# Attention in a fused kernel: order of the norm, of the first loads and of the weights' splitting

## The chip, the cores and the metric

One core of a Trainium2 chip runs the kernel. Its engines work side by side, each in the order of its own program, and wait for each other by semaphores: PE (TensorE, matmuls), DVE (VectorE), ACT (ScalarE), POOL (GpSimd), and SP, which here only starts DMAs. The metric is the device time of one execution in microseconds (us), the median of several.

## The reference, cut to what matters

Two layers of cross attention and feed-forward network run over 64 sequences of 128 tokens with 256 values each. The change is in the first one alone:

```
x = x + _L0_xattn_ref(ctx_1024, _layernorm(x), Wq, Wkv, Wo, ln1_w, ln1_b, ln2_w, ln2_b)

# _L0_xattn_ref(x, latents, ...): 16 heads of 64, INNER = 1024
xn = _layernorm(x, ln1_w, ln1_b)
ln = _layernorm(latents, ln2_w, ln2_b)
q = ln @ Wq
k, v = split(concat([xn, ln], tokens) @ Wkv)     # 256 keys a sequence
w = softmax(q k^T / 8)                           # per head
out = (w v) @ Wo
```

`ctx_1024` gives the tokens `x` of this function, and the normed `x` of the model the latents; so the latents are normed twice. The three stages behind (routed experts, an alignment, a quantized convolution network) are not touched.

## The kernel before

`attention` works on 32 pairs of sequences, p = 0 to 31, and cuts the 16 heads into four quads. A round u handles one quad of one pair (u = 4p + i), as two units n = 2u and 2u + 1, one a sequence; there are 128 rounds. The rounds are a software pipeline: in round u, PE makes the scores of round u, weighs the values of round u - 1 (`weigh_values`), projects k, q and v of round u + 1, and turns (transposes) the probabilities of round u. All matmuls with weights are made in three passes over a high and a low part of each operand, so every operand is split: ACT writes the high part, and a subtraction makes the low part, on DVE for q, k and the heads, on POOL for the inputs (`low_inputs`).

PE's results go to seven PSUM banks taken in turn. The order of the takes is written out by hand (`take`), and each take waits until the bank's user of seven takes before is done; for q that is `q_split`, raised by DVE's `low_q`. The second half of `turn_probs(2u + 1)` takes the bank that held q of round u + 1.

In the first round of a pair (i = 0) the norm of the next pair is made: `norm_a` (statistics of x and ctx on DVE, after which POOL's `inverse_std` makes the reciprocal deviations), `norm_b` (subtract and multiply, statistics of the latents), `norm_c` (second norm of the latents). In that round PE also makes the output of the pair before (`output`, 24 matmuls a sequence), and it ends with `turn_inputs`, which transposes the normed inputs of the next pair and waits for `normed`. ACT's `split_inputs` follows.

In the opening, SP loads 8 sequences of x, the norm columns, ctx of the first pair, and six pieces of 512 KB of weights (Wq, then Wkv's k and v halves) through four stages that lie in the yet empty end of `x_all`. DVE makes both parts of each piece (`split_weight`: a copy, L525, and a subtraction, L526). PE projects q, k, then v. Two pieces of Wo follow in the first round: DVE splits them between `row_max` and `invert`, and POOL's divide (L650) of the probabilities waits for `invert`.

Of the kernel before, what the change touches and what calls it, by code (L numbers as in the profile page):

```python
# [71 lines left out]
def attention(nc, dve_step, pool_step, x_all, ident, half, x, ctx, wq, wkv, wo, ln_cols):  # L72
# [10 lines left out]
    X_SETS = (range(0, 1), range(1, 2), range(2, 4), range(4, 8))  # L83
    STAGES, PER_STAGE = 4, INNER // DIM
    FREE_XC = (SEQS - STAGES * PER_STAGE) // XC
    MO = INNER // P
    with Stage(nc, "attention") as st:
# [28 lines left out]
        const_made, w_split = st.sems("const_made", "weights_split")  # L116
# [56 lines left out]
        for b in range(2):  # L173
            take("in", b, kv_scaled, 2 * b + 2)
        take("q", 0, q_split, 1)
        for c in range(2):
            take("k", c, k_split, c + 1)
        for c in range(2):
            take("v", c, v_copied, c + 1)
# [24 lines left out]
        def x_set(c):  # L204
            return next(i for i, chunks in enumerate(X_SETS) if c in chunks)

        def load_x(sp, c):
            sp.dma_start(x_all[:, XC * c:XC * c + XC, :], x[XC * c:XC * c + XC].rearrange("b t d -> t b d")
                         ).then_inc(x_loaded[x_set(c)], 16)

        def sp_program(sp):
            load_x(sp, 0)
            sp.dma_start(cols[:, :, :], ln_cols).then_inc(cols_loaded, 16)
# [21 lines left out]
            for c in range(FREE_XC, SEQS // XC):  # L235
                load_x(sp, c)
# [3 lines left out]
        def pe_program(pe):  # L240
# [58 lines left out]
            def project_v(c):  # L299
# [3 lines left out]
                pe.wait_ge(kv_split, 4 * p + 4)  # L303
# [66 lines left out]
            for c in range(2):  # L370
                project_v(c)
# [22 lines left out]
        def act_program(act):  # L394
# [61 lines left out]

            for b in range(2):
                split_inputs(b)
            high_q(0)
            for c in range(2):  # L460
                high_k(c)
            for c in range(2):
                copy_v(c)
            for u in range(ROUNDS + 1):
# [9 lines left out]
                if more:  # L474
# [3 lines left out]
                    copy_v(n + 3)  # L478
                if late_input(u) is not None:
                    split_inputs(late_input(u))  # L480

        def dve_program(dve):
# [18 lines left out]
            def norm_a(p):  # L501
                xs, cs, ls = pair(p)
                if 2 * p % XC == 0:
                    c = x_set(2 * p // XC)
                    dve.wait_ge(x_loaded[c], 16 * len(X_SETS[c]))
# [16 lines left out]
            def split_weight(n):  # L522
                src, hi, lo = staged[n]
                dve.wait_ge(stage_loaded[n % STAGES], 16 * (n // STAGES + 1))
                dve_step(dve, dve.tensor_copy(hi, stage_of(n)))  # L525
# [60 lines left out]
            for u in range(ROUNDS + 1):  # L586
# [18 lines left out]
                if norm_next:  # L605
                    norm_b(p + 1)
# [11 lines left out]
        def pool_program(pool):  # L618
# [23 lines left out]
            for b in range(2):  # L642
                low_inputs(b)
            for u in range(ROUNDS):
                p, i = divmod(u, QUADS)
                if p + 1 < PAIRS and not i:
                    inverse_std(p + 1, 0, 4)
                for n in (2 * u, 2 * u + 1):
# [3 lines left out]
                                       ).then_inc(divided, 1)  # L652
# [1525 lines left out]
```

## Time and profile before

| | |
|---|---|
| median of 3 runs | 3593.19 us (3592.61 to 3593.66) |
| the profiled execution | 3592.0 us, span 3590.3 us |
| PE busy | 3148.0 us, 88% of the span |
| DVE busy | 2499.0 us, 70% |
| ACT busy | 1830.2 us, 51% |
| POOL busy | 1352.1 us, 38% |

The span runs from the first to the last instruction of the profiled execution, and the rest of its time lies around it. Attention takes the time from 0 to about 1880 us. In the timelines the first number is the start in us from the span's start, the second how long the instruction or the merged run of them (xcount) took; square brackets tell how long the engine was idle before and who released it. PEld is PE's weight load.

### The profile page before, as it was taken

How to read it: one execution, taken by the hardware profiler on the slowest of the kernel's cores; microseconds unless marked ns; L12 is line 12 of the kernel's file. 1: busy time of each engine (PE TensorE's matmuls, PEld its weight loads, DVE VectorE, ACT ScalarE, POOL GpSimd, SP SyncE). 2: the span in 40 equal slices, each digit the busy share in tenths (PEclk: the TensorE clock that was granted, in tenths of full speed). 3: DMA queues.
4: the chain of work that ended last, by engine and by line, in shares of the span. 5: the costliest groups of instructions: out<-in, count | busy, mean ns of one | idle time of the engine just before them, and what ended most of it. 6: DMA issues, size and time to landing. Idle time of an engine off the chain costs nothing. (4 is left out here: it accounts for less than half of the span.)

```text
span 3590.3 us, 63845 instructions
## 1 busy us (share of the span) xinstructions
PE 3148.0 (88%) x23236; PEld 2704.7 (75%) x23236; DVE 2499.0 (70%) x5380; ACT 1830.2 (51%) x4693; POOL 1352.1 (38%) x1116
## 2 busy tenths in 40 slices
PE   6999999999999999999997999999999811177876
PEld 5888888888888888888886888888888710055655
DVE  6666666676666667676655665665664979789997
ACT  4555555556555555556553333333333612199996
POOL 2333333333333333333322333333333200068887
PEclk9999999999999999999998999999999955598888
DMA  4000000000000000000002101111101740001101
GB/s 150 4 7 5 7 7 4 7 4 7 4 7 4 7 7 4 7 4 7 4 1 78 48 32 41 49 30 43 48 25 48 215 103 0 12 30 36 38 29 35
DMA packets 104166, 107.96 MB, mean 30 GB/s; under 512 B 7857, under 2 KB 85169, under 8 KB 103857
## 3 DMA queue, kind: packets, MB, share of 16 engines
q1 hardware_dynamic: 103856, 103.88, 9.9%
q8 instruction: 189, 3.10, 0.4%
q14 instruction: 121, 0.98, 0.1%
HBM read 90.75 MB, written 13.11 MB: 29 GB/s over the span
## 5 line engine op out<-in xcount | busy, mean ns | idle before, releaser
L650 POOL TENSOR_TENSOR attention_prob<-attention_prob,attention_inv_sums 128x1024 f32<-128x1024 f32 x256 | 481.3, 1902 | 388.3 <-DVE attention_inv_sums L556 388.3
L442 ACT ACTIVATE attention_prob<-attention_turns,attention_neg_max 128x256 f32<-128x256 f32 x1024 | 468.5, 482 | 172.5 <-DVE attention_neg_max L547 172.5
L1097 POOL TENSOR_TENSOR experts_hidden_lo<-experts_weighed,experts_hidden_hi 128x512 fp32r<-128x512 f32 x192 | 252.0, 1313 | 551.9 <-ACT experts_hidden_hi L920 551.9
L563 DVE COPY attention_probT<-attention_turns 128x512 f32<-128x512 f32 x512 | 329.2, 684 | 151.5 <-PE attention_turns L329 151.5
L547 DVE TENSOR_REDUCE attention_neg_max<-attention_turns 128x2 f32<-128x512 f32 x512 | 317.8, 683 | 46.0 <-PE attention_turns L319 45.0
L920 ACT ACTIVATE experts_hidden_hi<-experts_weighed 128x512 fp32r<-128x512 f32 x192 | 121.4, 632 | 424.2 <-DVE experts_weighed L1049 424.2
L433 ACT COPY attention_v<-attention_turns 128x512 f32<-128x512 f32 x256 | 150.8, 589 | 330.0 <-PE attention_turns L263 330.0
L329 PE MATMUL attention_turns<-ident,attention_prob 128*128 128x128 f32 x2048 | 272.7, 274 | 42.2 <-DVE attention_q_lo L529 27.4
L329 PEld LDWEIGHTS attention_turns<-ident,attention_prob 128*128 128x128 f32 x2048 | 239.7, 141 | 85.8 <-DVE attention_q_lo L529 34.5
L1044 DVE TENSOR_TENSOR experts_silu<-experts_silu,experts_spread 128x512 f32<-128x512 f32 x128 | 89.3, 698 | 260.7 <-ACT experts_silu L914 259.6
L637 POOL TENSOR_TENSOR attention_kv_lo<-attention_kv_full,attention_kv_hi 128x256 fp32r<-128x256 f32 x128 | 96.2, 752 | 456.7 <-ACT attention_kv_hi L411 456.6
L345 PE MATMUL attention_heads_out<-attention_probT,attention_v 128*64 128x128 f32 x4096 | 251.8, 276 | 1.0 <-DVE attention_probT L563 1.0
L407 ACT ACTIVATE attention_kv_full<-attention_turns,attention_ln_cols 128x128 f32<-128x128 f32 x256 | 102.3, 449 | 270.2 <-PE attention_turns L256 269.4
L345 PEld LDWEIGHTS attention_heads_out<-attention_probT,attention_v 128*64 128x64 f32 x4096 | 220.9, 137 | 18.2 <-DVE attention_probT L563 1.2
L556 DVE RECIPROCAL attention_inv_sums<-attention_row_sums 128x4 f32<-128x4 f32 x256 | 44.5, 174 | 265.9 <-ACT attention_prob L442 265.9
L442 ACT ACTIVATION_READ_ACCUMULATOR attention_prob<-attention_turns,attention_neg_max 128x1 f32 x1024 | 219.5, 214 | 0.0
L853 PE MATMUL experts_out<-experts_down_hi,experts_hidden_hi 128*128 128x256 f32 x768 | 217.6, 283 | 0.6 <-POOL experts_hidden_lo L1097 0.6
L853 PE MATMUL experts_out<-experts_down_hi,experts_hidden_lo 128*128 128x256 f32 x768 | 217.3, 283 | 0.0
L853 PE MATMUL experts_out<-experts_down_lo,experts_hidden_hi 128*128 128x256 f32 x768 | 216.9, 282 | 0.0
L295 PE MATMUL attention_turns<-attention_kv_hi,attention_wkv_hi 128*128 128x512 f32 x512 | 215.1, 420 | 0.0
L263 PE MATMUL attention_turns<-attention_wkv_hi,attention_kv_hi 128*128 128x512 f32 x512 | 213.1, 416 | 0.0
L529 DVE SCALAR_TENSOR_TENSOR attention_k_lo<-attention_turns,attention_k_hi 128x512 fp32r<-128x512 f32 x256 | 176.6, 690 | 44.7 <-ACT attention_k_hi L425 40.3
(265 smaller groups left out, 9883.0 us busy)
## 6 DMA issues: line engine op xcount, KB each, us to landing
experts_spread<-shares SPq DMA_DIRECT2D x256, 128.0 KB, 3.0
x_all<-in_x SPq DMA_DIRECT2D x8, 1024.0 KB, 10.4
attention_ctx<-in_ctx SPq DMA_DIRECT2D x32, 256.0 KB, 2.8
distance_ctx<-in_ctx SPq DMA_DIRECT2D x16, 512.0 KB, 4.4
distance_ctxT<-in_ctxT SPq DMA_DIRECT2D x32, 256.0 KB, 4.8
weights_ctx<-in_ctx SPq DMA_DIRECT2D x16, 512.0 KB, 3.9
out<-conv_x_out SPq DMA_DIRECT2D x15, 512.0 KB, 3.0
dist<-distance_dist SPq DMA_DIRECT2D x16, 256.0 KB, 2.5
```

The source lines that it names most:

```text
L263: made = pe.matmul(out, left[l](k), right[r](k), start=n == 0, stop=n == 3 * KD - 1)
L295: made = pe.matmul(bank[:, :].rearrange("p (e c t) -> p c e t", e=2, c=2), wkv_p[l][:, k, w:w + P], (kv_hi, kv_lo)[r][p % 2][:, k, :, :, : ...
L329: made = pe.transpose(bank[:, (2 * h + t) * P:(2 * h + t + 1) * P], prob[n % 2][:, 2 * g + h, t * P:(t + 1) * P], ident[:, :])
L345: made = pe.matmul(heads_out[o * HEAD:(o + 1) * HEAD, (QT * e + m) * TOK:(QT * e + m + 1) * TOK], v[:, home, e, t, h, :], probT[e][:, h, t ...
L433: act.copy(v[:, 0:2 + pj % 2:1 + pj % 2, e, t, :, :].rearrange("p q h c -> p q (h c)"), bank_of("v", c)[:, :].rearrange("p (q c) -> p q c" ...
L442: made = act.activation(prob[n % 2][:, h, :], bank_of("s", 2 * n + e)[:, m * 256:(m + 1) * 256], ACT.Exp, bias=neg_max[:, n % 2, 2 * e + m ...
L529: return dve.scalar_tensor_tensor(lo, view, scale, hi.bitcast(F32), ALU.mult, ALU.subtract)
L547: made = dve.tensor_reduce(neg_max[:, n % 2, 2 * e:2 * e + 2], bank_of("s", 2 * n + e)[:, :].rearrange("p (h c) -> p h c", h=2), AX.X, ALU ...
L563: dve.tensor_copy(probT[n % 2][:, 2 * g:2 * g + 2].rearrange("p h t c -> p (h t c)"), bank_of("t", 2 * n + g)[:, :]).then_inc(p_copied, 1)
L650: pool.tensor_tensor(prob[n % 2][:, :, :], prob[n % 2][:, :, :], inv[:, n % 2, :].unsqueeze(2).broadcast_to([P, QH, 2 * TOK]), ALU.mult).t ...
L853: made = pe.matmul(out_ps[i // 2][:, (i % 2) * DIM:(i % 2 + 1) * DIM], l[n % 3][:, i * TOK:(i + 1) * TOK], down_w[r][:, m, :], start=t == ...
L1097: pool.tensor_tensor(hid_lo[n % 3][:, :], weighed[n % 2], hid_hi[n % 3][:, :].bitcast(F32), ALU.subtract).then_inc(hid_split, 1)
```

## The change

It is in `attention` alone and leaves every value computed as it is.

- The norm of the next pair: in rounds with i = 0, DVE now does `low_q`, `low_k` and the copy of the first unit's probabilities, then `norm_b`, the second copy, `norm_c`. In the first round `norm_a` comes behind the first copy too, and POOL makes the first reciprocal deviations behind the divides.
- Smaller first loads: x comes as sequences 0 and 1, later 2 to 7, then eights (`X_LOADS`); sequences 8 and up wait for somewhat other groups of loads (`X_SETS`).
- The weights come in another order, v, q, k, and ACT makes their high parts (`high_weight`), DVE their low parts (`low_weight`), laced into the first norm. PE projects v first and needs only one sequence's inputs for each of its first parts. DVE also makes the low parts of the first pair's inputs (`low_first_inputs`).
- The output weights are split when the first round ends.

```diff
-    X_SETS = (range(0, 1), range(1, 2), range(2, 4), range(4, 8))
+    X_LOADS = ((0, 2), (2, XC), *((c, c + XC) for c in range(XC, SEQS, XC)))
+    X_SETS = ((0,), (1,), (2, 3, 4), (5, 6, 7, 8))
+    X_FIRST = {X_LOADS[loads[0]][0]: i for i, loads in enumerate(X_SETS)}
...
-        for src, dst, c in ((wq, wq_p, 0), (wkv, wkv_p, 0), (wkv, wkv_p, INNER)):
+        for src, dst, c in ((wkv, wkv_p, INNER), (wq, wq_p, 0), (wkv, wkv_p, 0)):
...
-        WQ, WK, WV, WO = KD, 2 * KD, 3 * KD, 3 * KD + 2
+        WV, WQ, WK, WO = KD, 2 * KD, 3 * KD, 3 * KD + 2
...
         def sp_program(sp):
+            load_x(0)
             load_ctx(0)
-            for n in range(WV):
+            sp.dma_start(cols[:, :, :], ln_cols).then_inc(cols_loaded, 16)
+            for n in range(WK):
                 load_weight(n)
-            for c in range(1, FREE_XC):
-                load_x(sp, c)
+            load_x(1)
             load_ctx(1)
-            for n in range(WV, WO):
+            for n in range(WK, WO):
                 load_weight(n)
+            for n in range(2, FREE_LOADS):
+                load_x(n)
...
             def project_v(c):
-                pe.wait_ge(kv_split, 4 * p + 4)
+                pe.wait_ge(kv_split, 4 * p + 2 * e + 2)
...
+            for c in range(2):
+                project_v(c)
             project_q(0)
             for c in range(2):
                 project_k(c)
-            for c in range(2):
-                project_v(c)
...
+            def high_weight(n):
+                act.wait_ge(stage_loaded[n % STAGES], 16 * (n // STAGES + 1))
+                act.activation(staged[n][1], stage_of(n), ACT.Copy).then_inc(w_high, 1)
+
+            for n in range(STAGES):
+                high_weight(n)
             for b in range(2):
                 split_inputs(b)
+                high_weight(STAGES + b)
+            for c in range(2):
+                copy_v(c)
             high_q(0)
             for c in range(2):
                 high_k(c)
...
                     copy_v(n + 3)
+                if not u:
+                    for m in range(WK, WO):
+                        high_weight(m)
...
+            def low_weight(n):
                 src, hi, lo = staged[n]
+                dve.wait_ge(w_high, n + 1)
                 dve.tensor_tensor(lo, stage_of(n), hi.bitcast(F32), ALU.subtract).then_inc(w_split, 1)
...
+            def low_first_inputs(b):
+                for k in range(KD):
+                    dve.wait_ge(kv_high, 2 * b + k + 1)
+                    dve.tensor_tensor(kv_lo[0][:, k, :, b, :], kv_full[k][:, :, :],
+                                      kv_hi[0][:, k, :, b, :].bitcast(F32), ALU.subtract).then_inc(kv_split, 1)
+
             norm_a(0)
+            low_weight(0)
             norm_b(0)
+            low_weight(1)
             norm_c(0)
-            for n in range(WV):
-                split_weight(n)
+            low_weight(2)
+            low_first_inputs(0)
+            low_weight(3)
+            low_first_inputs(1)
+            low_weight(4)
+            low_weight(5)
             low_q(0)
...
                     row_max(n + 1)
-                    if not u:
-                        for m in range(WV, WO):
-                            split_weight(m)
-                    if norm_next:
+                    if norm_next and u:
                         norm_a(p + 1)
                     invert(n)
                     invert(n + 1)
...
                 if u:
                     low_heads(u - 1)
-                if norm_next:
-                    norm_b(p + 1)
                 if more:
                     low_q(u + 1)
                     low_k(n + 3)
                 if u < ROUNDS:
                     copy_probs(n)
+                    if not u:
+                        norm_a(1)
+                    if norm_next:
+                        norm_b(p + 1)
+                    copy_probs(n + 1)
                     if norm_next:
                         norm_c(p + 1)
-                    copy_probs(n + 1)
+                if not u:
+                    for m in range(WK, WO):
+                        low_weight(m)
...
             inverse_std(0, 1, 2)
-            for b in range(2):
-                low_inputs(b)
             for u in range(ROUNDS):
                 p, i = divmod(u, QUADS)
-                if p + 1 < PAIRS and not i:
+                if p + 1 < PAIRS and not i and u:
                     inverse_std(p + 1, 0, 4)
                 ...
+                if not u:
+                    inverse_std(1, 0, 4)
```

## Rows read from the trace of the kernel before

**Rows 1.** The page's busy time and share of each engine, whole span.

```profile
PE 3148.0 (88%) x23236; PEld 2704.7 (75%) x23236; DVE 2499.0 (70%) x5380; ACT 1830.2 (51%) x4693; POOL 1352.1 (38%) x1116
```

**Rows 2.** Waits on PE, 0 to 1900 us: total us, times, longest us.

```profile
PE attention_turns L329 <- DVE attention_q_lo L529: 27.4, 30, 0.9
```

**Rows 3.** Timeline of DVE, a round with norm: start, us, engine, line, operation.

```profile
1027.28 2.76 DVE L497 TENSOR_SCALAR attention_latents<-x_all,attention_mean_var,attention_rstd 128x256 f32<-128x256 f32 x2
...
1031.68 0.66 DVE L529 SCALAR_TENSOR_TENSOR attention_q_lo<-attention_turns,attention_q_hi 128x512 fp32r<-128x512 f32 x1
...
1032.85 1.28 DVE L563 COPY attention_probT<-attention_turns 128x512 f32<-128x512 f32 x2
```

**Rows 4.** Timeline of DVE, 0 to 62 us.

```profile
7.60 0.75 DVE L489 BATCH_NORM_STATS2 attention_raw_stats<-x_all 128x6 f32<-128x256 f32 x2 [7.60 <-DMA attention_ctx<-in_ctx]
...
11.01 0.73 DVE L497 TENSOR_SCALAR attention_latents<-x_all,attention_mean_var,attention_rstd 128x256 f32<-128x256 f32 x2 [1.58 <-POOL attention_rstd L628]
...
14.62 0.74 DVE L497 TENSOR_SCALAR attention_latents<-attention_latents,attention_mean_var,attention_rstd 128x256 f32<-128x256 f32 x2 [1.16 <-POOL attention_rstd L628]
...
15.99 1.23 DVE L526 TENSOR_TENSOR attention_wq_lo<-x_all,attention_wq_hi 128x1024 fp32r<-128x1024 f32 x1
...
42.76 0.69 DVE L525 CAST attention_wo_hi<-x_all 128x1024 fp32r<-128x1024 f32 x1 [6.14 <-DMA x_all<-in_wo]
```

**Rows 5.** Timeline of POOL, the same round as rows 3.

```profile
1026.10 3.79 POOL L650 TENSOR_TENSOR attention_prob<-attention_prob,attention_inv_sums 128x1024 f32<-128x1024 f32 x2
```

**Rows 6.** Timeline of PE, the same round as rows 3.

```profile
1030.88 0.60 PE L329 MATMUL attention_turns<-ident,attention_prob 128*128 128x128 f32 x4
1032.39 0.66 PE L329 MATMUL attention_turns<-ident,attention_prob 128*128 128x128 f32 x4 [0.91 <-DVE attention_q_lo L529]
1033.08 0.36 PE L360 MATMUL attention_turns<-attention_wo_hi,attention_attT_hi 128*128 128x256 f32 x1
...
1038.90 0.27 PE L256 MATMUL attention_turns<-ident,attention_ctx 128*128 128x128 f32 x1
```

**Rows 7.** Timeline of PE, the round that starts at 59.11 us.

```profile
59.11 0.39 PE L319 MATMUL attention_turns<-attention_k_hi,attention_q_hi 64*128 64x256 f32 x2
...
70.55 1.03 PE L329 MATMUL attention_turns<-ident,attention_prob 128*128 128x128 f32 x8
71.42 0.27 PE L256 MATMUL attention_turns<-ident,attention_ctx 128*128 128x128 f32 x1
```

**Rows 8.** GB/s of the DMAs, 0 to 16 us, in 40 slices of 0.4 us.

```profile
GB/s 0 0 0 0 36 108 69 148 338 317 381 387 389 364 357 386 358 376 430 379 451 389 420 379 451 358 430 420 318 92 0 0 0 0 0 0 0 0 0 0
```

**Rows 9.** Timeline of ACT, 0 to 62 us.

```profile
7.00 1.28 ACT L407 ACT_TABLE_LOAD   x1 [7.00 <-DMA attention_ln_cols<-in_ln_cols]
```

**Rows 10.** ACT's groups by form: busy us, mean ns, idle us before.

```profile
L407 ACT ACTIVATE attention_kv_full<-attention_turns,attention_ln_cols 128x128 f32<-128x128 f32 x256 | 102.3, 449 | 270.2 <-PE attention_turns L256 269.4 <-POOL attention_kv_lo L637 0.8
...
L894 ACT ACTIVATE experts_xT_hi<-experts_xT 128x1024 fp32r<-128x1024 f32 x16 | 16.7, 1041 | 0.0
```

**Rows 11.** Timeline of PE, 0 to 62 us.

```profile
15.41 0.48 PE L256 MATMUL attention_turns<-ident,attention_ctx 128*128 128x128 f32 x1 [15.41 <-DVE attention_latents L497]
...
23.65 0.58 PE L263 MATMUL attention_turns<-attention_kv_hi,attention_wq_hi 128*128 128x256 f32 x1 [6.27 <-POOL attention_kv_lo L637]
...
26.38 0.63 PE L295 MATMUL attention_turns<-attention_kv_hi,attention_wkv_hi 128*128 128x512 f32 x1
...
28.82 0.40 PE L295 MATMUL attention_turns<-attention_kv_hi,attention_wkv_hi 128*128 128x512 f32 x1
...
33.10 0.39 PE L319 MATMUL attention_turns<-attention_k_hi,attention_q_hi 64*128 64x256 f32 x2
...
51.68 1.97 PE L329 MATMUL attention_turns<-ident,attention_prob 128*128 128x128 f32 x8 [11.16 <-POOL attention_prob L650]
```

**Rows 12.** Windows of 1 us: each engine's busy us (x), then PEclk, DMA, GB/s.

```profile
45.00:46.00 1.00, 0.00 (x0) 0.00 (x0) 0.97 (x2) 0.00 (x0) 0.00 (x0) 0.88 0.00 0
...
56.00:57.00 1.00, 1.00 (x9) 0.80 (x7) 1.00 (x2) 0.59 (x1) 0.52 (x1) 1.00 0.00 0
```

More of the change, by code:

```diff
@@ L81, in attention @@
     XC = 8
-    X_SETS = (range(0, 1), range(1, 2), range(2, 4), range(4, 8))
+    X_LOADS = ((0, 2), (2, XC), *((c, c + XC) for c in range(XC, SEQS, XC)))
+    X_SETS = ((0,), (1,), (2, 3, 4), (5, 6, 7, 8))
+    X_FIRST = {X_LOADS[loads[0]][0]: i for i, loads in enumerate(X_SETS)}
     STAGES, PER_STAGE = 4, INNER // DIM
-    FREE_XC = (SEQS - STAGES * PER_STAGE) // XC
+    FREE_LOADS = 1 + (SEQS - STAGES * PER_STAGE) // XC
     MO = INNER // P
@@ L115, in attention @@
         ctx_loaded, cols_loaded = st.sems("ctx_loaded", "cols_loaded")
-        const_made, w_split = st.sems("const_made", "weights_split")
+        const_made, w_high, w_split = st.sems("const_made", "weights_high", "weights_split")
         stats_made, rstd_made, normed = st.sems("stats_made", "rstd_made", "normed")
@@ L174, in attention @@
             take("in", b, kv_scaled, 2 * b + 2)
+        for c in range(2):
+            take("v", c, v_copied, c + 1)
         take("q", 0, q_split, 1)
@@ L177, in attention @@
             take("k", c, k_split, c + 1)
-        for c in range(2):
-            take("v", c, v_copied, c + 1)
         for u in range(ROUNDS + 1):
@@ L202, in bank_of, with load_x @@
             return turns[take_at[kind, n] % len(turns)]
[L204 to L209, printed above, removed]
         def sp_program(sp):
-            load_x(sp, 0)
-            sp.dma_start(cols[:, :, :], ln_cols).then_inc(cols_loaded, 16)
+            def load_x(n):
+                lo, hi = X_LOADS[n]
+                sp.dma_start(x_all[:, lo:hi, :], x[lo:hi].rearrange("b t d -> t b d")).then_inc(
+                    x_loaded[next(i for i, loads in enumerate(X_SETS) if n in loads)], 16)
             def load_ctx(p):
@@ L224, in load_weight @@
                 sp.dma_start(stage_of(n), staged[n][0]).then_inc(stage_loaded[n % STAGES], 16)
+            load_x(0)
             load_ctx(0)
-            for n in range(WV):
+            sp.dma_start(cols[:, :, :], ln_cols).then_inc(cols_loaded, 16)
+            for n in range(WK):
                 load_weight(n)
-            for c in range(1, FREE_XC):
-                load_x(sp, c)
+            load_x(1)
             load_ctx(1)
-            for n in range(WV, WO):
+            for n in range(WK, WO):
                 load_weight(n)
+            for n in range(2, FREE_LOADS):
+                load_x(n)
             sp.wait_ge(w_split, WO)
-            for c in range(FREE_XC, SEQS // XC):
-                load_x(sp, c)
+            for n in range(FREE_LOADS, len(X_LOADS)):
+                load_x(n)
             for p in range(2, PAIRS):
@@ L369, in pe_program @@
                 project_k(c)
-            for c in range(2):
-                project_v(c)
             for u in range(ROUNDS + 1):
@@ L455, in high_heads @@
                                ).then_inc(att_high, 1)
+            def high_weight(n):
[3 more added lines that the diff above has]
+                high_weight(n)
             for b in range(2):
                 split_inputs(b)
+                high_weight(STAGES + b)
+            for c in range(2):
+                copy_v(c)
             high_q(0)
@@ L461, in act_program @@
                 high_k(c)
-            for c in range(2):
-                copy_v(c)
             for u in range(ROUNDS + 1):
@@ L502, in norm_a @@
                 xs, cs, ls = pair(p)
-                if 2 * p % XC == 0:
-                    c = x_set(2 * p // XC)
-                    dve.wait_ge(x_loaded[c], 16 * len(X_SETS[c]))
+                if 2 * p in X_FIRST:
+                    i = X_FIRST[2 * p]
+                    dve.wait_ge(x_loaded[i], 16 * len(X_SETS[i]))
                 dve.wait_ge(ctx_loaded, 16 * (p + 1))
@@ L520, in norm_c @@
                 normalise(ls, ls, mv[1], rstd[1]).then_inc(normed, 1)
-            def split_weight(n):
+            def low_weight(n):
                 src, hi, lo = staged[n]
-                dve.wait_ge(stage_loaded[n % STAGES], 16 * (n // STAGES + 1))
-                dve_step(dve, dve.tensor_copy(hi, stage_of(n)))
+                dve.wait_ge(w_high, n + 1)
                 dve.tensor_tensor(lo, stage_of(n), hi.bitcast(F32), ALU.subtract).then_inc(w_split, 1)
```

## The prediction, made before the change was built or timed

> **What bounds the kernel now.** I read the engines' busy time first: PE (TensorE) is busy for 88% of the span, far above DVE (VectorE) and POOL (GpSimd) [rows 1]. So I looked at PE's idle time in attention with the view of waits, restricted to PE and to the first 1900 us. It has one line that repeats: 30 times, `turn_probs` (L329) waits for DVE's `low_q` (L529), 27.4 us in all, 0.9 us at most [rows 2]. Thirty is the number of rounds with u >= 1 in which the next pair's norm is made. The rest of PE's idle time in attention lies before the second round. Nothing else in attention repeats.
>
> The timeline of PE and DVE shows how the repeated wait arises. The last four transposes of `turn_probs(n+1)` need the PSUM bank that held q; it is free when `low_q` is done. DVE runs its program in order and has `norm_b` ahead of `low_q`. The first two subtractions of `norm_b` take 2.76 us there instead of 0.73 [rows 3, 4], while POOL runs its divides from 1026.10 to 1029.89 [rows 5]. `low_q` starts at 1031.68 and ends at 1032.34; PE resumes at 1032.39 [rows 3, 6].
>
> **The size of the wait.** From the first of these transposes to the first matmul behind them it is 1033.08 - 1030.88 = 2.20 us [rows 6]; in a round without the wait, 71.42 - 70.55 = 0.87 us [rows 7]. The difference is 1.33 us, more than the 0.91 shown as idle, because the view starts counting only when the modelled (pipelined) ends are past. I take 1.33, and keep 0.91 as the lower bound.
>
> **Part 1: the norm behind the queries.** Nothing is added or removed, DVE's order changes. `low_q` and `low_k` follow `low_heads` at 1027.3 and end about 1028.7 (two of 0.7). The bank is then free some 2.8 us before PE asks for it at 1031.3. Behind them comes `copy_probs(n)`: its transposes start about 2.3 before 1030.88, so the copy runs 1029.3 to 1030.6. `norm_b` starts at 1030.6, behind the divides. From `norm_b`'s start to `norm_c`'s start takes 3.61 us where nothing disturbs it, 1.16 of it waiting for POOL [rows 4]; `copy_probs(n+1)`, 1.28 us [rows 3], now lies in that wait, so `norm_c` starts near 1034.3 and ends near 1035.0. PE needs it for `turn_inputs`, at 1038.90 before [rows 6] and 1037.6 with the wait gone: 2.6 us in hand. The banks that `copy_probs(n+1)` frees near 1034.3 are wanted by the next scores at 1038.1. I find no new wait. Gain: 30 x 1.33 = 39.9 us; bounds 30 x 0.91 = 27.4 and 39.9.
>
> The Trainium skill (SBUF — State Buffer, "Who interferes with whom") says that a tensor_scalar in a 2-port mode and a GpSimd instruction shut each other out for a whole instruction, whoever is first. By that rule the 2.76 us are a block and go away when `norm_b` moves behind the divides; without the rule (2.76 kept) `norm_c` would end near 1037.1, still ahead of 1037.6, and the sum would be the same.
>
> **Part 2: the opening, up to the first score.** DVE starts at 7.60, when 1.31 MB (x, 8 sequences, and ctx) are in [rows 4]. By the row of GB/s [rows 8] 1.31 MB have moved by 6.4, so landing lags by about 1.1 us. Now only 0.52 MB are ahead: moved by 4.3, so DVE starts near 5.4 (5.0 to 5.6). But `low_weight(0)` stands before `norm_b` and waits for ACT, which waits for the first weight: 1.05 MB, moved by 5.7, landed near 6.8. The one table load takes 1.28 us and began at 7.00, at a DMA's landing [rows 9]; I place it behind the weight's wait (lower bound: before it, 1.28 less). Then 1.04 for ACT's copy [rows 10] and 1.23 for DVE's subtraction [rows 4]: `norm_b` starts near 10.4 instead of 11.01. `low_weight(1)` (1.23) fills the 1.16 wait for POOL. So `norm_c` starts near 14.1 and the transposes, 0.79 behind it as before (14.62 to 15.41 [rows 4, 11]), near 14.9. In `low_weight(1)`, DVE reads two SBUF tensors while POOL computes the rstd that is waited for; if POOL had to wait out the subtraction, 1.1 us more. Bounds 13.6 and 16.0; I take T = 15.2.
>
> Before, POOL made the low inputs, and the queries began 8.24 us after the transposes (15.41 to 23.65 [rows 11]). Now `project_v` needs only the first sequence: four transposes (1.1), two ACT scalings of two and two copies, six of about 0.45 [rows 10], and a short DVE subtraction: T + 4.1. From the first projection to the first score PE works 33.0 - 23.65 = 9.35 us, with matmuls of 512 columns at 0.63 us each at first and 0.40 from 28.8 on [rows 11]; this start comes after idle time too, so I keep 9.35. V first takes the first 5 us, in which the second sequence's input parts (about T + 7.5) and the K weights (about T + 9.9) are ready before Q and K want them. K is now last, so its high part (0.6) and low part (0.66 [rows 3]) and the hand-overs are exposed: 1.4 us that V covered before. First score: T + 4.1 + 9.35 + 1.4 = T + 14.9 = 30.1, against 33.10 [rows 11]. Gain 3.0 (bounds 2.2 and 4.6).
>
> **Part 3: the first round.** Before, `invert` stood behind the output weights, whose DMA landed at 42.76 [rows 4]; the round from score to score took 59.11 - 33.10 = 26.0 us [rows 7, 11]. Now with S the first score: PE is ready for the first transposes at S + 7.4 (before, it stopped 11.16 us ahead of 51.68 [rows 11], and 33.10 was S), the divide is done by then (no DMA ahead of it), and DVE copies the first probabilities from about S + 8.3 to S + 9.6. Then `norm_a(1)` to `norm_b` 3.41 us (7.60 to 11.01 [rows 4]), `norm_b` to `norm_c` 3.7 (with the copy in it), `norm_c` 0.74, transposes about 0.5: next score at S + 18.1. Gain 7.9, give or take 1. PE stands idle from S + 10.5 to S + 17.6, 7.1 us. Before, PE stopped near 40.5 and the granted clock fell to 0.50 (the 1.2 GHz level) at about 45.9, and rose to 1.00 about 4.3 us after PE resumed at 51.68 [rows 11, 12]. The same should happen here, with 4.3 us at half rate inside the second round: -2.1 us (bounds 0 and -2.2). The output weights' two low parts (1.23 each) make the second round's maxima about 1 us late; the divide there has more than 2 us before its transposes, so nothing. ACT's two high parts (1.04 each) lie in its idle time before `split_inputs`. The smaller x loads add one DMA issue, behind the weights. What is moved behind them, x 2 to 7 and ctx 1, is wanted near 40, and all has moved by then.
>
> Opening and first round together: 3.0 + 7.9 - 2.1 = 8.8 us (bounds 5 and 13).
>
> **Sum.** 39.9 + 8.8 = 48.7 us. The profiled execution took 3592.0 us (span 3590.3 and 1.7 around it) and becomes 3543.3; it lies 1.2 below the median of the runs, 3593.19, so I predict 3544.5 us. Everything behind attention is merely earlier.
>
> **Rivals.**
> *Only the idle time shown comes back.* The 1.33 measures start to start; if part of it is PE's own restart that stays at that place, each round gives 0.91: 3593.2 - 27.4 - 8.8 = 3557.0. For: the view counts 27.4. Against: a round without the wait has 0.87 at that place. Chance 0.12.
> *The opening gives nothing.* DVE's strict order behind the weights eats the earlier start and the norm holds PE in the first round for 8 us more: 3593.2 - 39.9 = 3553.3. For: `low_weight(0)` waits for DMA and ACT. Against: `invert` no longer waits for a DMA. Chance 0.09.
> *The wait moves within the round.* Something else frees the bank late and the 30 waits stay at their old size: 3593.2 - 8.8 = 3584.4. Against: DVE has 2.8 us in hand. Chance 0.03, and 0.02 that this goes with an opening that gives little, so that the time is the same.
> *Slower: the norm chain takes over PE's wait.* Place: `turn_inputs` at 1037.6. If `norm_b`'s subtractions now hit POOL work for 3 us each, `norm_c` ends near 1041.2, PE waits 3.6 us, 30 x (3.6 - 1.3) = 69 less 8.8: 3653. It decides from an end of `norm_c` past 1039.2, 4.2 us later than I have it. Against: POOL's divides end at 1029.89 [rows 5], before `norm_b` starts. Chance 0.02.
> *The forecast* has 0.72, with its own range 3540 to 3550.
>
> **Range and chances.** 3538 to 3560 holds the forecast, the first two rivals and the bounds of the opening. 0.2% is 7 us, about what a measurement of this kernel can tell from no change. Faster 0.96, same 0.02, slower 0.02.
>
> **What the changed profile would show.** The 30 waits of L329 for L529 are gone, and the round with the norm is 1.3 us shorter each time. `norm_b`'s first pair of subtractions takes 0.73. The first score is near 30, the second round's near 48, with about 7 us of idle PE before it and a granted clock of 0.5 around its start. Wrong would be: a new repeated wait of PE for L497 or L563, `low_weight(0)` much later than 10, or a first round over 20 us.

## The result and the profile after

The changed kernel takes 3541.3 us (median of 4, 3539.67 to 3543.53) against 3592.9 us: ratio 0.9857, 95% interval 0.984 to 0.9874. The forecast was 3544.5 us, so a gain of 48.7 us was expected and 51.6 us were measured. The profiled execution of the changed kernel is its slowest run, 3543.53 us with a span of 3541.8 us.

The page's head shows the same work (as [rows 1]) in a shorter span:

```profile
span 3541.8 us, 63842 instructions
...
PE 3136.5 (89%) x23236; PEld 2706.4 (76%) x23236; DVE 2437.3 (69%) x5376; ACT 1838.3 (52%) x4701; POOL 1345.0 (38%) x1112
```

The 30 waits of PE for `low_q` (L329 for L529, [rows 2]) are gone; from 60 to 1800 us the view of waits on PE is empty. This is PE in a round with the norm, as [rows 6]:

```profile
97.04 1.04 PE L329 MATMUL attention_turns<-ident,attention_prob 128*128 128x128 f32 x8
...
99.31 1.03 PE L329 MATMUL attention_turns<-ident,attention_prob 128*128 128x128 f32 x8
100.10 0.36 PE L360 MATMUL attention_turns<-attention_wo_hi,attention_attT_hi 128*128 128x256 f32 x1
```

The eight transposes run on without a break, and the first output matmul follows 0.79 us after their start, where it was 2.20 us. DVE in the same round, as [rows 3]:

```profile
95.71 0.68 DVE L538 SCALAR_TENSOR_TENSOR attention_q_lo<-attention_turns,attention_q_hi 128x512 fp32r<-128x512 f32 x1
...
97.74 1.29 DVE L572 COPY attention_probT<-attention_turns 128x512 f32<-128x512 f32 x2 [0.58 <-PE attention_turns L329]
98.95 0.73 DVE L507 TENSOR_SCALAR attention_latents<-x_all,attention_mean_var,attention_rstd 128x256 f32<-128x256 f32 x2
...
101.31 1.26 DVE L572 COPY attention_probT<-attention_turns 128x512 f32<-128x512 f32 x2
102.56 0.74 DVE L507 TENSOR_SCALAR attention_latents<-attention_latents,attention_mean_var,attention_rstd 128x256 f32<-128x256 f32 x2
```

`low_q` runs at 95.71, ahead of the norm. `norm_b`'s first two subtractions take 0.73 us instead of 2.76, since POOL's divides are over. `norm_c` is done at 103.3, in time for `turn_inputs`. From score to score, each of the 30 rounds with norm and output takes 18.60 us instead of 20.00; from the third round on the others are unchanged at 12.40 to 12.85 us, one at 18.16.

The opening on DVE, as [rows 4], and on ACT, as [rows 9]:

```profile
4.44 0.75 DVE L499 BATCH_NORM_STATS2 attention_raw_stats<-x_all 128x6 f32<-128x256 f32 x2 [4.44 <-DMA attention_ctx<-in_ctx]
...
8.59 1.23 DVE L535 TENSOR_TENSOR attention_wkv_lo<-x_all,attention_wkv_hi 128x1024 fp32r<-128x1024 f32 x1 [2.33 <-ACT attention_wkv_hi L459]
9.73 0.73 DVE L507 TENSOR_SCALAR attention_latents<-x_all,attention_mean_var,attention_rstd 128x256 f32<-128x256 f32 x2
...
12.10 1.19 DVE L535 TENSOR_TENSOR attention_wkv_lo<-x_all,attention_wkv_hi 128x1024 fp32r<-128x1024 f32 x1
14.21 0.73 DVE L507 TENSOR_SCALAR attention_latents<-attention_latents,attention_mean_var,attention_rstd 128x256 f32<-128x256 f32 x2 [0.93 <-POOL attention_rstd L651]
```

```profile
0.78 1.28 ACT L459 ACT_TABLE_LOAD   x1 [0.78 <-PEq L2194]
7.50 1.06 ACT L459 ACTIVATE attention_wkv_hi<-x_all 128x1024 fp32r<-128x1024 f32 x1 [5.43 <-DMA x_all<-in_wkv]
```

The norm starts at 4.44 instead of 7.60, but then DVE waits 2.33 us for ACT's first high part, which started when the first weight landed at 7.50. So `norm_b` starts at 9.73, only 1.3 us earlier than before. The table load ran at 0.78, long before.

POOL's two reciprocal deviations:

```profile
6.44 0.24 POOL L650 TENSOR_SCALAR attention_var_eps<-attention_mean_var 128x4 f32<-128x4 f32 x1 [4.87 <-DVE attention_mean_var L502]
...
12.27 1.11 POOL L650 TENSOR_SCALAR attention_var_eps<-attention_mean_var 128x2 f32<-128x2 f32 x1 [4.46 <-DVE attention_mean_var L502]
```

The second L650 takes 1.11 us. It started with `low_weight(1)` (12.10 to 13.29) and ended right behind it; the first took 0.24.

PE in the opening, as [rows 11]:

```profile
15.00 0.47 PE L256 MATMUL attention_turns<-ident,attention_ctx 128*128 128x128 f32 x1 [15.00 <-DVE attention_latents L507]
...
19.07 0.80 PE L263 MATMUL attention_turns<-attention_wkv_hi,attention_kv_hi 128*128 128x512 f32 x1 [2.10 <-DVE attention_kv_lo L590]
19.66 0.63 PE L263 MATMUL attention_turns<-attention_wkv_lo,attention_kv_hi 128*128 128x512 f32 x1
...
25.95 0.40 PE L295 MATMUL attention_turns<-attention_kv_hi,attention_wkv_hi 128*128 128x512 f32 x1
...
47.80 0.45 PE L256 MATMUL attention_turns<-ident,attention_ctx 128*128 128x128 f32 x1 [6.90 <-DVE attention_latents L507]
...
48.82 0.59 PE L319 MATMUL attention_turns<-attention_k_hi,attention_q_hi 64*128 64x256 f32 x2
```

The first score starts at 30.34 instead of 33.10, the second round's at 48.82 instead of 59.11. Ahead of the second round's inputs (47.80) PE is idle for 6.9 us. A matmul of 512 columns takes 0.63 us at first and 0.40 later; the change of pace comes at 24.77. The granted clock, as [rows 12], falls to 0.50 in that gap and is back at about 52:

```profile
45.00:46.00 1.00, 0.00 (x0) 0.00 (x0) 0.97 (x5) 0.00 (x0) 0.14 (x1) 0.61 0.00 0
52.00:53.00 1.00, 1.00 (x22) 1.00 (x20) 1.00 (x2) 1.00 (x5) 0.13 (x1) 0.98 1.05 303
```

### The profile page after: what moved, and what is told of

Same layout as the page of the kernel before. It is cut to its first block and busy times, and to the rows that moved or that the text cites. A ratio compares the mean times of both kernels' runs of the same rounds, so it can differ in the third digit from the quotient of the medians.

```text
span 3541.8 us, 63842 instructions
## 1 busy us (share of the span) xinstructions
PE 3136.5 (89%) x23236; PEld 2706.4 (76%) x23236; DVE 2437.3 (69%) x5376; ACT 1838.3 (52%) x4701; POOL 1345.0 (38%) x1112
## 5 line engine op out<-in xcount | busy, mean ns | idle before, releaser
L329 PEld LDWEIGHTS attention_turns<-ident,attention_prob 128*128 128x128 f32 x2048 | 240.2, 141 | 39.7 <-POOL attention_prob L671 4.2
L329 PE MATMUL attention_turns<-ident,attention_prob 128*128 128x128 f32 x2048 | 266.1, 273 | 3.7 <-POOL attention_prob L671 3.7
L345 PE MATMUL attention_heads_out<-attention_probT,attention_v 128*64 128x128 f32 x4096 | 253.7, 277 | 0.8 <-DVE attention_probT L572 0.8
L345 PEld LDWEIGHTS attention_heads_out<-attention_probT,attention_v 128*64 128x64 f32 x4096 | 222.7, 137 | 18.2 <-DVE attention_probT L572 1.2
```

Source lines behind the costliest of these rows:

```text
L329: made = pe.transpose(bank[:, (2 * h + t) * P:(2 * h + t + 1) * P], prob[n % 2][:, 2 * g + h, t * P:(t + 1) * P], ident[:, :])
L345: made = pe.matmul(heads_out[o * HEAD:(o + 1) * HEAD, (QT * e + m) * TOK:(QT * e + m + 1) * TOK], v[:, home, e, t, h, :], probT[e][:, h, t ...
```

## The experiments

All comparisons are with the kernel before. Single executions of one kernel differ by up to 7.6 us (e1), so the small effects below are read from the traces. The time of each round is the distance between the first score matmuls (L319) of successive rounds.

**The norm's order alone (e1_norm_only).** In the kernel before, `norm_b` and `norm_c` are moved for u >= 1 only:

```diff
-                if norm_next:
+                if norm_next and not u:
                     norm_b(p + 1)
...
                     copy_probs(n)
-                    if norm_next:
+                    if norm_next and u:
+                        norm_b(p + 1)
+                        copy_probs(n + 1)
+                        norm_c(p + 1)
+                    elif norm_next:
                         norm_c(p + 1)
-                    copy_probs(n + 1)
+                        copy_probs(n + 1)
```

> The kernel before with one edit: from the second pair's rounds on, `norm_b` stands behind `copy_probs(n)` and `norm_c` behind `copy_probs(n+1)`; the opening and the first round are those of before. Theory: the wait of `turn_probs` for `low_q` is the whole gain of the steady rounds, and it comes back start to start: the round with the norm falls from 20.0 to 18.6 us, 30 x 1.40 = 42 us, so 3551 us. Rival, only the idle time shown comes back: 30 x 0.91 = 27.4 us, 3565.5 us. Rival, the gain needs the new opening too: the 30 waits stay, 3593 us.

Measured: 3548.4 us (3546.52 to 3554.12) against 3593.58, ratio 0.9878 (0.9865 to 0.9892). No PE wait is left between 60 and 1800 us and the round with the norm takes 18.60 us. The last round's first score is at 1826.70 instead of 1869.75, 43.05 us earlier, of which 42.0 are 30 x 1.40 and the rest is the opening's spread. Both rivals are out.

**The opening alone (e2_opening_only).** In the changed kernel, `norm_b` goes back ahead of `low_q` for u >= 1:

```diff
+                if norm_next and u:
+                    norm_b(p + 1)
                 if more:
                     low_q(u + 1)
                     low_k(n + 3)
                 if u < ROUNDS:
                     copy_probs(n)
+                    if norm_next and u:
+                        norm_c(p + 1)
                     if not u:
                         norm_a(1)
-                    if norm_next:
-                        norm_b(p + 1)
+                        norm_b(1)
                     copy_probs(n + 1)
-                    if norm_next:
-                        norm_c(p + 1)
+                    if not u:
+                        norm_c(1)
```

> The changed kernel with the norm put back ahead of the queries in all rounds but the first. Theory: the two parts add. The 30 waits of 0.91 us are back, the first score is at 30.3 and the second round's first score at 48.8 us as in the changed kernel, and the time is 3592.9 less some 8.9 to 9.6 us, 3583 to 3584 us. Rival, the opening's gain is lost later on when PE is held by DVE in every pair: 3590 us or more.

Measured: 3581.86 us (3581.4 to 3582.08), ratio 0.9969 (0.9958 to 0.9981). The view of waits on PE from 60 to 1800 us has its one line again:

```profile
PE attention_turns L329 <- DVE attention_q_lo L538: 27.4, 30, 0.9
```

The last round's first score is at 1861.26, 8.49 us earlier than before. In attention the parts add: 43.05 + 8.49 = 51.5, and with both it is 51.1 (1869.75 - 1818.64). The medians do not quite: 45.2 + 11.7 = 56.9 against 51.6. In the profiles, the parts' gains exceed that of both by 7.4 us. Of these, 0.4 arise up to the last round's first score and 1.3 in that round (see below). The other 5.7 lie in the stages behind attention, which no edit touches: they took 1695.1 us before, 1692.1 in e1, 1692.6 in e2, and 1695.4, 1692.0 and 1691.9 in three profiles of the changed kernel. So most of what the profiles differ by is a spread between executions.

**Behind the queries, but under the divides (e3_norm_before_copies).** The changed kernel with `norm_b` between `low_k` and `copy_probs(n)`:

```diff
                     low_k(n + 3)
+                if norm_next and u:
+                    norm_b(p + 1)
                 if u < ROUNDS:
                     copy_probs(n)
+                    if norm_next and u:
+                        norm_c(p + 1)
...
-                    if norm_next:
-                        norm_b(p + 1)
+                        norm_b(1)
                     copy_probs(n + 1)
-                    if norm_next:
-                        norm_c(p + 1)
+                    if not u:
+                        norm_c(1)
```

> The changed kernel, but from the second pair on `norm_b` stands between `low_k` and `copy_probs(n)`, and `norm_c` between the two copies. So the norm is behind the queries and still partly under POOL's divides. Theory: only the place behind `low_q` counts. `norm_b`'s first subtractions wait about 1.2 us for the divide to end, no PE wait comes back, and the time is that of the changed kernel within 1 us, 3541 us. Rival, the place behind the divides is what counts: part of the wait comes back at the copies, and the round with the norm takes 19 to 20 us, 3553 us or more.

Measured: 3541.09 us (3539.2 to 3545.83), ratio 0.9853 (0.9838 to 0.9869): the changed kernel's time. POOL's divides and DVE's first subtractions in a round with the norm:

```profile
95.95 3.74 POOL L674 TENSOR_TENSOR attention_prob<-attention_prob,attention_inv_sums 128x1024 f32<-128x1024 f32 x2
...
98.49 1.67 DVE L507 TENSOR_SCALAR attention_latents<-x_all,attention_mean_var,attention_rstd 128x256 f32<-128x256 f32 x2
```

The pair of subtractions takes 1.67 us, 0.94 more than undisturbed; its first 1.20 us lie beside the divide, which ends at 99.69. The round takes 18.60 us all the same. So it is the place behind `low_q` that counts, not the one behind the divides.

**A first load of 8 sequences (e4_first_load_8).**

```diff
-    X_LOADS = ((0, 2), (2, XC), *((c, c + XC) for c in range(XC, SEQS, XC)))
-    X_SETS = ((0,), (1,), (2, 3, 4), (5, 6, 7, 8))
+    X_LOADS = tuple((c, c + XC) for c in range(0, SEQS, XC))
+    X_SETS = ((0,), (1, 2, 3), (4, 5, 6, 7))
...
-            load_x(1)
             load_ctx(1)
```

> The changed kernel with a first load of x of 8 sequences, as before the change. Theory: `norm_b` of the first pair is gated by the landing of the first weight (through ACT's and DVE's first splitting steps); 0.79 MB more ahead of it at some 375 GB/s make it 2.1 us later, the first score is near 32.4 instead of 30.3, and the time is 3543.4 us. Rival, the load's size is hidden: first score at 30.3 still, 3541.3 us. Rival, the start of the norm (7.5 instead of 4.4) counts in full: first score at 33.4, 3544.4 us.

Measured: 3542.79 us (3539.95 to 3545.6), ratio 0.986 (0.9847 to 0.9873). DVE and ACT in its opening:

```profile
7.34 0.75 DVE L498 BATCH_NORM_STATS2 attention_raw_stats<-x_all 128x6 f32<-128x256 f32 x2 [7.34 <-DMA attention_ctx<-in_ctx]
...
10.98 0.73 DVE L506 TENSOR_SCALAR attention_latents<-x_all,attention_mean_var,attention_rstd 128x256 f32<-128x256 f32 x2
```

```profile
8.75 1.06 ACT L458 ACTIVATE attention_wkv_hi<-x_all 128x1024 fp32r<-128x1024 f32 x1 [6.69 <-DMA x_all<-in_wkv]
```

The norm starts 2.9 us later (7.34), `norm_b` only 1.3 us (10.98), and the first score is at 30.82. ACT's first high part started at 8.75. But with the small load, in unaltered openings, it started at 7.50, 7.67, 8.01, 8.04, 8.60, 8.87 and 9.02 in seven executions, and their first scores came between 29.66 and 31.81. My 2.1 us is not there in this profile, nor are 3.1; a cost below the spread of 1.5 us cannot be excluded. Nor can the medians tell: two of the four runs took 3540 us and two 3545.5.

**The changed kernel again (e0_after_again), and a third time (e9_after_third).**

> The changed kernel once more, unaltered, as a measure for the three beside it, and to see whether the granted clock falls again in attention's last round, as it did in its first profile (from 1.00 to 0.50 at 1827 us, a round later than the last full one) and did not before. Theory, the fall is a matter of the single execution: it is there in some profiles and not in others, and costs about 2.4 us where it is. Rival, the changed kernel's order brings it: it is there in every profile of it. Time 3540 to 3543 us.

> The changed kernel a third time, unaltered, beside the one above, to compare their medians on the same chip and to see a third clock record of its last round. Time 3539 to 3542 us. Theory: the fall of the granted clock in the last round differs from execution to execution of the same kernel, so the time from the last round's first score to the expert stage's first transposes is not 27.8 or 29.2 us each time but anything from 25.4 to 29.2. Rival: it is a property of the kernel and is 27.8 to 29.2 us again.

Measured: 3540.85 us (3538.44 to 3542.02), ratio 0.9857 (0.9842 to 0.9871), and 3539.81 us (3539.25 to 3540.64), ratio 0.9856 (0.9842 to 0.9869). The first score was at 29.67 and 30.02. The clock fell in the last round in both; what that shows is told with the last experiment.

**The next norm's statistics earlier.** Two kernels, each the changed one with `norm_a(1)` elsewhere in the first round. In e5_norm_a_first it is ahead of both `invert`, and POOL's `inverse_std(1, 0, 4)` ahead of the divides, as in all other rounds (the `and u` and the two `if not u` blocks are taken out). In e6_norm_a_between:

```diff
                     invert(n)
+                    if not u:
+                        norm_a(1)
                     invert(n + 1)
...
                     copy_probs(n)
-                    if not u:
-                        norm_a(1)
...
                                        ).then_inc(divided, 1)
-                if not u:
-                    inverse_std(1, 0, 4)
+                    if not n:
+                        inverse_std(1, 0, 4)
```

> The changed kernel with `norm_a(1)` ahead of both `invert` in the first round and POOL's reciprocal deviations ahead of the divides, as in all other rounds. Theory: PE's idle time in the first round hangs on the norm chain, which starts earlier; PE waits about 1.3 us for the divide, `turn_inputs` starts near 45.3 instead of 47.8, the idle time before it is near 3 us, too short for the granted clock to fall, and the second round takes 12.8 instead of 14.2 us: 3.9 us less in all. Rival, the later divides delay the chain by as much: the same time. Rival, the clock falls anyway: 2.5 us less.

> The changed kernel with `norm_a(1)` between the two `invert` of the first round, where DVE waits 1.65 us for ACT, and POOL's reciprocal deviations between the two divides. Theory: no divide is late, `turn_inputs` starts near 44.5 instead of 47.8, the granted clock does not fall, and the second round takes 12.8 us: 4.7 us less than the changed kernel. Rival, the clock falls anyway: 3.3 us less. Rival, POOL's steps and DVE's block each other: no gain.

Measured: 3540.37 us (3537.4 to 3541.91), ratio 0.9853 (0.9837 to 0.987), and 3538.63 us (3536.72 to 3542.45), ratio 0.9853 (0.9838 to 0.9867). The first round takes 15.94 and 15.12 us instead of 18.47, so 2.5 and 3.35 us are won there. In the medians they are 0.5 and 2.2 us below e0_after_again, which ran on the same chip beside them, with ranges that overlap, so the gain is shown by the traces alone. PE in e6 ahead of the second round, and its clock:

```profile
43.76 0.45 PE L256 MATMUL attention_turns<-ident,attention_ctx 128*128 128x128 f32 x1 [3.30 <-DVE attention_latents L507]
```

```profile
42.00:43.00 1.00, 0.00 (x0) 0.00 (x0) 1.00 (x3) 0.00 (x0) 0.76 (x2) 1.00 0.00 0
44.00:45.00 1.00, 1.00 (x6) 0.67 (x7) 1.00 (x2) 0.11 (x1) 0.00 (x0) 0.50 0.07 16
46.00:47.00 1.00, 1.00 (x13) 1.00 (x12) 0.51 (x1) 0.97 (x4) 0.73 (x1) 0.50 0.08 9
47.00:48.00 1.00, 1.00 (x20) 0.87 (x18) 1.00 (x3) 0.48 (x2) 0.63 (x1) 1.00 0.73 153
```

PE is idle for 3.3 us only, and yet the granted clock falls to 0.50 (1.2 GHz). It is back at 47, and the second round takes 13.85 us (14.00 in e5), not 12.84. In e5 the clock falls 0.1 us behind the end of a gap of 3.0 us. My theory held for the chain and fell for the clock: the rival "the clock falls anyway" is what the traces show.

**The weights' low parts behind the norm (e7_weights_behind_norm).**

```diff
             norm_a(0)
-            low_weight(0)
             norm_b(0)
-            low_weight(1)
             norm_c(0)
+            low_weight(0)
+            low_weight(1)
             low_weight(2)
```

> The changed kernel with the first three `low_weight` behind `norm_c(0)` instead of laced into the first norm. Theory: the first norm is held by the first weight (DVE idle 2.33 us and 1.23 us of work ahead of `norm_b`) and POOL's first step is held by `low_weight(1)` on the port that both use (1.11 us instead of 0.23). Both go: `norm_b` starts near 7.9 instead of 9.73, the transposes near 12.3 instead of 15.0, and, since the weights' later pieces now wait for the split to free their stage, the first score near 27.8 instead of 30.3: 2.5 us less. Rival, the freed stages come too late: K's weights hold PE and the first score stays at 30: same time.

Measured: 3539.77 us (3537.77 to 3541.72), ratio 0.9855 (0.984 to 0.9869). POOL and PE in the opening:

```profile
10.34 0.23 POOL L650 TENSOR_SCALAR attention_var_eps<-attention_mean_var 128x2 f32<-128x2 f32 x1 [2.57 <-DVE attention_mean_var L502]
```

```profile
12.20 0.47 PE L256 MATMUL attention_turns<-ident,attention_ctx 128*128 128x128 f32 x1 [12.20 <-DVE attention_latents L507]
...
16.57 0.79 PE L263 MATMUL attention_turns<-attention_wkv_hi,attention_kv_hi 128*128 128x512 f32 x1 [2.39 <-DVE attention_kv_lo L590]
...
23.93 0.47 PE L295 MATMUL attention_turns<-attention_kv_hi,attention_wkv_hi 128*128 128x512 f32 x1 [0.80 <-DVE attention_wkv_lo L535]
```

`norm_b` starts at 7.81, the second L650 takes 0.23 us again, and the transposes start at 12.20. The projection of v starts at 16.57 instead of 19.07. But K's weights now come late: PE waits 0.80 us for their low part at 23.93. First score 28.39: of 2.8 us won for the transposes 1.95 are left against the first profile of the changed kernel, and 1.3 and 1.6 against the other two. That is 0.6 to 1.2 short of the 2.5 expected; the order of events is as expected. The median is 1.1 us below e0_after_again, with ranges that overlap.

**Both (e8_both):** the edits of e6 and e7 together.

> The changed kernel with both re-orderings that showed a gain in the trace: `norm_a(1)` between the two `invert` (and POOL's reciprocal deviations between the divides), and the first three `low_weight` behind `norm_c(0)`. Theory: the two lie one behind the other on the same path and add. First score near 28.4 and the first round 15.1 us long, so the second round's first score near 43.5 instead of 48.1 to 49.4 in the changed kernel; the clock falls to 0.50 around it all the same and the second round takes 13.9 us. Time 5 us less than the changed kernel, 3536 us. Rival: what is won is taken back in the last round, where the granted clock fell in every profile but the one of before, by a different amount each time: the median stays at 3539 us or above.

Measured: 3535.17 us (3534.37 to 3537.8), ratio 0.9842 (0.9829 to 0.9856). PE:

```profile
12.15 0.47 PE L256 MATMUL attention_turns<-ident,attention_ctx 128*128 128x128 f32 x1 [12.15 <-DVE attention_latents L507]
...
27.98 0.39 PE L319 MATMUL attention_turns<-attention_k_hi,attention_q_hi 64*128 64x256 f32 x2 [1.46 <-issue]
...
42.08 0.30 PE L256 MATMUL attention_turns<-ident,attention_ctx 128*128 128x128 f32 x1 [3.29 <-DVE attention_latents L507]
```

First score 27.98, first round 14.65, second round 14.35, so its first score is at 42.63, more than 5 us earlier than in any profile of the changed kernel. The median is 4.6 us below that of e9_after_third, which ran on the same chip beside it, and the ranges of the two do not touch. It is the fastest kernel of the study.

**The kernel before again (e10_before_again).**

> The kernel before, unaltered, once more with a profile. In its first profile the granted clock stayed at 1.00 through attention's last round (25.4 us from the round's first score to the expert stage's first transposes), while it fell there in all eleven profiles of changed kernels (25.95 to 29.2 us). Theory: the fall is a matter of the single execution and can come to the kernel before as well: 25.4 to 29.2 us here. Rival: the kernel before never falls, and the changed kernel pays about 2.4 us there for its own order: 25.4 us again.

Measured: one run, 3592.54 us. Its last round:

```profile
1876.00:1877.00 1.00, 1.00 (x7) 1.00 (x6) 0.57 (x2) 0.00 (x0) 1.00 (x1) 0.50 0.08 16
...
1879.00:1880.00 1.00, 0.28 (x3) 0.03 (x1) 1.00 (x2) 0.00 (x0) 0.00 (x0) 1.00 0.00 0
```

The clock fell here too, for 3.4 us, and the stretch took 25.89 us. The stretch, from the last round's first score to the expert stage's first transposes, in all profiles:

| kernel | us |
|---|---|
| before; e10_before_again | 25.42; 25.89 |
| e1_norm_only; e2_opening_only | 25.95; 25.99 |
| after, e0_after_again, e9_after_third | 27.78; 29.22; 27.69 |
| e3; e4; e5; e6; e7; e8 | 29.20; 27.79; 27.77; 27.70; 29.21; 28.82 |

Neither of my two theories holds whole. The fall is not the changed kernel's own, since the kernel before has it. But chance alone hardly explains it either: the nine profiles with both parts of the change took 1.7 to 3.8 us longer there than the four with one or none. PE in the first profile of the kernel before, where the clock stayed at 1.00 through these gaps:

```profile
1876.28 1.09 PE L329 MATMUL attention_turns<-ident,attention_prob 128*128 128x128 f32 x8 [2.93 <-POOL attention_prob L650]
```

And in the first profile of the changed kernel:

```profile
1820.28 1.97 PE L345 MATMUL attention_heads_out<-attention_probT,attention_v 128*64 128x128 f32 x32
...
1827.03 1.97 PE L329 MATMUL attention_turns<-ident,attention_prob 128*128 128x128 f32 x8 [0.76 <-POOL attention_prob L671]
1829.79 3.68 PE L345 MATMUL attention_heads_out<-attention_probT,attention_v 128*64 128x128 f32 x32 [0.78 <-DVE attention_probT L572]
```

The same 32 matmuls of L345 take 1.97 us at 1820.28 and 3.68 at 1829.79, in the fall. PE has gaps in this last round in every kernel (2.93, 0.76, 1.01 and 1.43 us in the kernel before, 2.94, 0.76, 0.78 and 1.42 here). The clock did not fall in them in the first profile of the kernel before; it fell for 3.4 us in e1, e2 and e10, and for 6.8 to 13.7 us in the nine others. Why is open.

## Why the prediction was right

- **The size of the wait** (1.33 us a round, 39.9 in all). Right in kind, low by 5%: 1.40 a round, 42.0 in all. The yardstick was off: I took a round in which the input transposes follow (0.87, [rows 7]); in the changed kernel the output matmuls follow at 0.79. The 0.91 of the view of waits [rows 6] was two thirds of what came back, so the first rival fell (e1, e3).
- **Part 1.** `low_q`'s place alone accounts for it (e1, e3). `norm_c` ends at 103.3 in that round and PE's `turn_inputs` starts at 105.93, so 2.6 us are in hand and PE has no wait, as worked out.
- **Part 2, the first score** (30.1 forecast, 30.34, 29.67 and 30.02 measured). The sum was right, but by luck: terms were wrong both ways and nearly cancelled. DVE started at 4.44, ahead of my 5.0 to 5.6, which made no difference, since it then waited for the weight. The table load was not behind the first weight's wait but at 0.78, 1.28 us less. The first weight landed at 7.5 to 9.0, not at 6.8. And POOL did have to wait out `low_weight(1)`: `norm_c` 0.93 us behind the end of that subtraction, where I had counted 0.3 of the possible 1.1. The 1.4 us for K's exposed low part came as expected (PE idle for 1.46 before the first score). My 9.35 us for PE's own work was not a fixed number: it took 9.8, 8.6 and 9.0 us in the three profiles, since the slow pace of the first matmuls ended 5.7, 3.1 and 3.9 us behind the first projection.
- **Part 3, the first round** (18.1 forecast, 18.48 measured, the gain 7.5 instead of 7.9). The chain is as predicted, idle PE 6.9 us (7.1).
- **The clock** (-2.1). It fell; the second round took 14.22, 15.30 and 13.84 us in three profiles of the changed kernel instead of 12.84, so -1.0 to -2.5, once beyond my bound of -2.2. That a shorter gap would have saved it, as e5 and e6 assumed, was wrong.
- **The sum.** By the last round's first score the profile gives 2.76 + 7.53 - 1.38 + 42.0 = 50.9 us, and 51.1 by its own times; my 48.7 is 2.2 less, nearly all of it the term of the wait. "Everything behind attention is merely earlier" held: those stages took 1695.4 after 1695.1 us. What was missed lies inside attention, whose last round took 27.78 instead of 25.42 us. The prediction said that the rest of PE's idle time in attention lay before the second round, which is wrong: the last round has 6.1 us of it in the kernel before, and it is there that the clock fell. The profiled execution gained 3592.0 - 3543.5 = 48.5 us; that this is nearly my 48.7 is luck, 2.2 too little and 2.4 too much. The medians differ by 51.6, as the other executions of the changed kernel were 1.9 to 3.9 us faster than the profiled one.
- **The other rivals.** The wait did not move (e1), the norm chain did not take over (the same 2.6 us in hand), and the opening gave 8.5 us, not nothing (e2).

The Trainium skill (SBUF — State Buffer, "Who interferes with whom") says that a DVE instruction with two SBUF inputs contends with a GpSimd instruction that reads SBUF. The trace agrees: L650 on POOL took 1.11 us beside `low_weight(1)` and 0.23 with it moved away (e7). For the 2.76 us of `norm_b` the rule of the block, as the prediction cites it, agrees too: the two subtractions ended at 1028.14 and 1030.04, each 0.15 us behind the end of one of POOL's two divides (1027.99 and 1029.89). They took 1.67 us when they started 1.20 us before the divides' end (e3), 0.73 behind them. That they ran in a 2-port mode is shown by no row.

## What to carry to other kernels

A wait in a full PE pipeline can cost more than the idle time shown: measure it start to start against the same successor in a round without it (here 1.40 against 0.91). In an engine that works in order, look for what stands ahead of the instruction that frees a bank or a buffer, and put what nobody waits for yet behind it; these were two moved calls and four fifths of the gain. In an opening, find the last of the things waited for before making the others earlier: the smaller load brought the norm 3 us forward, and the wait for a weight with its splitting took most of it back (e7 got it back by moving the splitting). Two errors that cancel look like a good forecast; compare each term.

## What the runs showed of the hardware that was not expected

- The granted clock fell to 0.50 between 2.2 and 5.2 us after PE had stopped ahead of the second round, in all thirteen profiles, and not at the same point in the same kernel: 5.2 us in the first profile of the kernel before and 2.2 in the second (e10), in gaps of 11.2 and 10.7 us. With a gap of 3.3 us (e6) it fell inside it, with 3.0 us (e5) 0.1 us behind its end. It was back 3.2 to 6.3 us after PE resumed. It fell also in attention's last round, whose gaps are 2.9 us and less.
- In the opening the granted clock reads 1.00 throughout, yet PE starts its matmuls of 512 columns 0.43 us apart at first and 0.23 later. The pace changed 3.1 to 5.9 us behind the first projection, and differently in the same kernel (5.7, 3.1 and 3.9 us), so it moves the first score about as much as the weight's landing: in seven profiles with the same opening, the first score came 10.1 to 11.4 us behind the first projection.
- ACT's one table load ran at 7.00, with a DMA's landing, where two waits stood ahead of the first activation, and at 0.78 where one stood.
- The same first weight landed anywhere between 7.50 and 9.02 us in seven executions with the same opening.
